# Moving the projections' SiLU multiplications from VectorE to GpSimd, with an extra ScalarE pass

## The reference

```python
x = x + ga * mamba(ln(x) * (1 + ca) + sa)              # A: conv, SiLU, a scan over 16 states
x = x + gb * moe_top2(ln(x) * (1 + cb) + sb)           # B: routed experts, width 64
x = x + ga1 * gated_delta(ln(x) * (1 + ca1) + sa1)     # C
x = x + gb1 * attention_moe(ln(x) * (1 + cb1) + sb1)   # D: attention, 8 dense experts, width 512
```

```python
def short_conv(x, w):          # w: 4 taps for each channel
    xp = jnp.pad(x, ((0, 0), (Kc - 1, 0), (0, 0))).transpose(0, 2, 1)
    y = lax.conv_general_dilated(xp, w[:, None, :], (1,), 'VALID', feature_group_count=w.shape[0])
    return jax.nn.silu(y.transpose(0, 2, 1))
q = short_conv(x @ Wq, conv_q)   # 8 heads of 128 channels
k = short_conv(x @ Wk, conv_k)   # 8 heads of 128 channels
v = short_conv(x @ Wv, conv_v)   # 8 heads of 32 channels
```

## Time and profile before

| | us |
|---|---|
| median of 3 executions | 2813.87 |
| lowest and highest | 2811.92, 2821.78 |
| span of the profiled execution | 2813.2 |
| PE busy | 2441.0 |
| DVE (VectorE) busy | 2212.7 |
| ACT (ScalarE) busy | 1200.1 |
| POOL (GpSimd) busy | 549.1 |

### The profile page before, as it was taken

How to read it: one execution, slowest core, us unless ns; L and a number is a source line. 1 busy time by engine, 2 the same in 40 slices (tenths; PEclk the granted TensorE clock), 3 DMA queues, 4 the chain that set the end, 5 groups by cost and what they waited for, 6 DMA issues and landing times.

```text
span 2813.2 us, 61085 instructions
## 1 busy us (share of the span) xinstructions
PE 2441.0 (87%) x22584; PEld 1893.0 (67%) x22584; DVE 2212.7 (79%) x5136; ACT 1200.1 (43%) x2697; POOL 549.1 (20%) x497
## 2 busy tenths in 40 slices
PE   3688989888898988989888898988989889898997
PEld 2466768667686766768667586766758667686776
DVE  6677897878879887787878879887887978879742
ACT  3332536344353543436444353543536444253512
POOL 2122221122222022121112222022121112222010
PEclk7789999999999999999999999999999999999998
DMA  4000000000000000000000000000000000000000
GB/s 132 4 2 3 7 4 1 8 3 8 3 7 2 3 8 3 7 3 4 5 3 8 3 7 2 3 8 3 7 3 5 4 3 8 3 7 2 1 6 3
DMA packets 24835, 21.46 MB, mean 8 GB/s; under 512 B 7218, under 2 KB 21571, under 8 KB 24531
## 3 DMA queue, kind: packets, MB, share of 16 engines
q1 hardware_dynamic: 24530, 17.26, 2.2%
HBM read 15.13 MB, written 2.13 MB: 6 GB/s over the span
## 4 chain that ended last, share of the span: by engine, by line
PE 32%; issue 32%; DVE 27%; POOL 4%; ACT 2%; DVEq 0%; POOLq 0%; ACTq 0%
DVE wide L1382 4%; DVE wide L1394 3%; PE banks L891 3%; PE banks L1198 3%; PE banks L1024 3%; PE banks L1188 3%; DVE wide L1402 3%; PE banks L1016 2%; PE banks L1052 2%; DVE inv L1570 2%; PE banks L1005 2%; DVE inv L1566 2%; PE banks L963 1%; PE banks L1065 1%; DVE inv L1557 1%
## 5 line engine op out<-in xcount | busy, mean ns | idle before, releaser
L1519 DVE SCALAR_TENSOR_TENSOR wide<-pad,conv,wide 128x256 f32<-128x256 f32 x864 | 370.0, 496 | 0.0
L561 POOL TENSOR_TENSOR wide<-wide 128x512 f32<-128x512 f32 x128 | 188.3, 1471 | 832.0 <-DVE wide L1402 472.0
L1394 DVE TENSOR_TENSOR_SCAN wide<-wide 128x1024 f32<-128x1024 f32 x128 | 292.9, 2288 | 1.9 <-ACT wide L667 0.3
L667 ACT ACTIVATE wide<-small,a_neg 128x255 f32<-128x255 f32 x512 | 216.0, 496 | 173.9 <-DVE wide L1394 173.0
L1044 PE MATMUL banks<-hideb,identb 128*128 128x512 bf16 x800 | 272.1, 403 | 0.0
L1188 PE MATMUL banks<-inv,up 128*128 128x256 f32 x1024 | 264.5, 387 | 0.0
L1198 PE MATMUL banks<-down,inv 128*128 128x128 f32 x2048 | 256.5, 276 | 0.0
L1198 PEld LDWEIGHTS banks<-down,inv 128*128 128x128 f32 x2048 | 248.7, 192 | 5.0
L796 ACT ACTIVATE inv<-banks,up1b 128x256 f32<-128x256 f32 x512 | 214.0, 480 | 52.0 <-PE banks L1188 51.5
L1024 PEld LDWEIGHTS banks<-inv,mats 64*64 64x64 f32 x5120 | 168.3, 139 | 63.9 <-issue 62.1
L1024 PEld LDWEIGHTS banks<-inv 64*64 64x64 f32 x5120 | 159.5, 135 | 67.4 <-issue 65.3
(11 more groups left out here) (280 smaller groups left out, 4933.4 us busy)
## 6 DMA issues: line engine op xcount, KB each, us to landing
gates_bc<-gate_rows SPq DMA_DIRECT2D x32, 128.0 KB, 2.9
x<-in_x SPq DMA_DIRECT2D x16, 128.0 KB, 2.1
up<-in_W SPq DMA_DIRECT2D x1, 2048.0 KB
out<-xn_y SPq DMA_DIRECT2D x16, 128.0 KB, 2.1
wide<-in_wmod SPq DMA_DIRECT2D x2, 384.0 KB, 5.6
con<-in_con SPq DMA_DIRECT2D x1, 724.0 KB, 4.7
w_k<-in_Wk SPq DMA_DIRECT2D x1, 512.0 KB
w_q<-in_Wq SPq DMA_DIRECT2D x1, 512.0 KB
```

The lines of the kernel that those rows point to most:

```text
L561: g.tensor_tensor(ypart[p % 2], r[:, 0:512], r[:, 512:1024], ALU.add).then_inc(a_yp.h, 1)
L667: last = s.activation(decay[st % 2][:, at + 1:at + T], dt[:, c, 1:T], ACT.Exp, scale=a_neg[:, c, st * SG + q:st * SG + q + 1])
L1394: v.tensor_tensor_scan(state[st % 2], decay[st % 2], drive[st % 2], 0.0, ALU.mult, ALU.add).then_inc(a_h.h, 1)
L1519: v.scalar_tensor_tensor(dst, src, w, dst, ALU.mult, ALU.add).then_inc(c_conv.h, 1)
```

## The change

The nine SiLU multiplications of each sample leave VectorE. GpSimd gets a `c_proj` of its own with them, as plain products of two tensors, and since a plain product cannot add the one, ScalarE adds it in a second instruction over the whole 128x512 tile, in place, which waits for its own tanh. The semaphore `c_th` counts to 18 instead of 9. On GpSimd the 12 steps of `c_proj` stand between `c_norm` and `c_gate`, so `c_gate` moves from the beginning of the stage to behind the last multiplication. The added wait of the next pass (`c_kq` in `a_norm`) is on GpSimd's own earlier work.

```diff
@@ TURNS
     "gpsimd": (
-        "yyxxyyyyyyxxxxxxxyxyxxyyxyxxx"),
+        "yyxxyyyyyyxxxxxxxyxyxxyyxyxxxxxxxxxxxxxxx"),
@@ signals
-        c_th = sig("c_tanh", 9); c_kq = sig("c_silu", 9); c_sq = sig("c_squares", 8)
+        c_th = sig("c_tanh", 18); c_kq = sig("c_silu", 9); c_sq = sig("c_squares", 8)
@@ gpsimd
                     g.wait_ge(mod_done, 1)
+                else:
+                    g.wait_ge(c_kq.h, c_kq.at(i - 1, 9))
...
+            def c_proj(i, m):
+                if 0 <= m - 3 < 9:
+                    n = m - 3
+                    if n == 0 and not isinstance(i, int):
+
+                        g.wait_ge(c_rms.h, c_rms.at(i - 1, 8))
+                    g.wait_ge(c_th.h, c_th.at(i, 2 * n + 2))
+                    g.tensor_tensor(kq[:, n] if n < 8 else v2, th1[n % 2], xc1[n % 3], ALU.mult).then_inc(c_kq.h, 1)
@@ scalar
                     s.activation(th1[m % 2], xc1[m % 3], ACT.Tanh, scale=0.5).then_inc(c_th.h, 1)
+                    s.wait_ge(c_th.h, c_th.at(i, 2 * m + 1))
+                    s.activation(th1[m % 2], th1[m % 2], ACT.Identity, bias=1.0).then_inc(c_th.h, 1)
@@ vector
             def c_proj(i, m):
-                if 0 <= m - 3 < 9:
-                    n = m - 3
-                    if n == 0 and not isinstance(i, int):
-
-                        v.wait_ge(c_rms.h, c_rms.at(i - 1, 8))
-                    v.wait_ge(c_th.h, c_th.at(i, n + 1))
-                    v.scalar_tensor_tensor(kq[:, n] if n < 8 else v2, th1[n % 2], 1.0, xc1[n % 3], ALU.add, ALU.mult).then_inc(c_kq.h, 1)
                 m -= 1
```

More of the change, by code:

```diff
@@ L606, in _ @@
             follow(g, TURNS["gpsimd"], dict(a_norm=a_norm, a_scan=a_scan, b_norm=lambda i: rstd(i, 1), b_root=b_root_, c_norm=lambda i: rstd(i, 2),
-                           c_gate=c_gate, c_gmask=c_gmask, c_roots=c_roots, c_unit=c_unit,
+                           c_proj=c_proj, c_gate=c_gate, c_gmask=c_gmask, c_roots=c_roots, c_unit=c_unit,
                            c_squares=c_squares, c_rms=c_rms_, d_norm=lambda i: rstd(i, 3)))
```

## The result

The change makes the kernel slower: 2903.52 us (median of 4, 2897.69 to 2908.35) against 2817.82 us (median of 4, 2811.92 to 2825.61). The ratio is 1.0304, with a 95% interval of 1.0279 to 1.0329, some 86 us. The span of the profiled execution went from 2813.2 to 2906.5 us. The forecast had the direction right and a size of 56 us.

What follows compares the result with a forecast made beforehand. TensorE, packed in the projections, was taken as the bound. 3.5 us for each of 15 passes (52.5) plus 3.6 for sample 0 made 56 us on the 2813.2 span, 2869.3, so 2870 us; range 2838 to 2903.

Steps and rivals of the forecast that it cites:

- 3.9 - 0.7 + 0.3 = 3.5 us a pass: Projections: later end of VectorE's last convolution, less delay taken up in the tail, plus waits of ScalarE and VectorE not coinciding.
- What bounds the kernel: Projections: TensorE packed, 32.00 of 32.00 us, VectorE nearly so; the start of the last sums of squares moves the pass's end.
- Part 2: GpSimd's products in the projections: eight fall on convolutions, each stopping VectorE 1.01 us; 8.1 us against 4.2 saved, 3.9 later.
- the upper bound: Most that one GpSimd product could cost VectorE: 1.27 us, the whole length of L561.
- The lower bound: Least that one GpSimd product could cost VectorE: nothing, if it always fell on a `d_mix` or a wait.
- Part 3: ScalarE in the projections: added instruction lengthens a step from 2.96 to 3.63 us, making ScalarE as full as VectorE.
- The rival in which ScalarE alone sets the pace: Projections: products meet no convolution, ScalarE costs 1.2 to 1.8 us a pass; about 2837 us, chance 0.13.
- the step without ReLUs: ScalarE between m = 5 and 6: the wait for the product is not hidden there, leaving about 0.5 us.
- Part 4: Last convolution's end to last sums of squares: 2.73 us becomes 2.0, taking up 0.7; 0.3 added back for waits.
- Part 5: `c_gate`, roots and masks after the projections: roots slip under 1 us against a cover of 3.7 us.
- Sample 0: Projections of the first sample, outside the 15 passes: 3.9 - 1.0 + 0.7 = 3.6 us slower, its tail growing.
- The rival's 2907 us: TensorE's clock falls in new projection gaps: some 5 us at low level cost 2.5 more, 6.0 a pass; chance 0.08.

Runs made afterwards that it cites:

- unread fills, no pass: Changed kernel with each GpSimd product replaced by fills that read nothing from SBUF, and ScalarE's added instruction left out: 2810.15 against 2819.56 us, 0.9974.
- the pass alone, warm: Kernel before plus only ScalarE's added instruction, products staying on VectorE, with 5 extra TensorE matmuls a sample holding the clock up: 2849.38 against 2819.56 us, 1.0115.
- unread fills and the pass: Changed kernel with each GpSimd product replaced by fills that read nothing from SBUF, ScalarE's added instruction kept: 2857.11 against 2819.56 us, 1.0129.
- products, no pass: Changed kernel with ScalarE's added instruction left out, so the one is not added: 2876.71 against 2813.81 us, 1.0217.
- fills reading one column, and the pass: Changed kernel with each GpSimd product replaced by fills and a tiny product reading one SBUF column: 2889.32 against 2813.81 us, 1.0268.
- changed, warm: Changed kernel plus 15 extra TensorE matmuls a sample ahead of the waits for squares, to hold the clock up: 2894.84 against 2819.56 us, 1.0267.
- changed, warm, second product let in: Changed kernel with 15 extra matmuls a sample, and VectorE made to wait within block 3's convolution for the second product: 2880.36 against 2817.61 us, 1.0208.
- changed, warm, products in halves: Changed kernel with 15 extra matmuls a sample, each GpSimd product cut in two of 128x256: 2911.57 against 2817.61 us, 1.0333.
- nine products more on the kernel before: Kernel before plus nine GpSimd products a sample, of constant tiles into a spare tile nobody reads: 2974.53 against 2813.81 us, 1.0570.
- the pass alone: Kernel before plus only ScalarE's added instruction, the product staying on VectorE as a plain product of two tensors: 2867.81 against 2813.81 us, 1.0199.

## Why the prediction was right about the direction and wrong about the size

In lengths at full clock, the runs give this account of a pass (the changed kernel itself has no pass without a low stretch):

| | us | over before |
|---|---|---|
| before | 35.87 | |
| unread fills, no pass | 35.87 | 0.0 |
| the pass alone, warm | 38.06 | 2.2 |
| unread fills and the pass | 38.08 | 2.2 |
| products, no pass | 39.04 | 3.2 |
| fills reading one column, and the pass | 39.91 | 4.0 |
| changed, warm | 40.86 | 5.0 |
| changed, warm, second product let in | 39.70 | 3.8 |
| changed, warm, products in halves | 41.42 | 5.5 |
| nine products more on the kernel before | 42.8 | 6.9 |

So a pass pays 2.2 us for ScalarE's added instruction, some 1.8 for GpSimd being held up by VectorE (39.91 - 38.08), some 1.0 for VectorE being stopped (40.86 - 39.91), and on top 42.56 - 40.86 = 1.7 for the low clock. The three differences are taken in this order, and another order would share out the 5.0 us a little differently. 5.0 x 15 = 75 us is what the passes of the warm kernel cost; its sample 0 costs 6.6 more, and its span is 85.3 us over the one before, though its median is 75. With the clock it is 6.7 x 15 = 100 us of length, plus 4.2 for sample 0, less the 15 us by which the stage between was shorter than before (120.3 against 121.3 us, 15 times): 89, against 93.3 of span. Of the 4 us left, 3 lie between the last sums and the next L1018.

**What failed** is the sum 3.9 - 0.7 + 0.3 = 3.5 us a pass, against 5.0 at full clock and 6.7 as it ran. The product that VectorE holds up stood in it at nothing and costs some 1.8 us. The tail stood in it with 0.4 us gained, and 0.6 were lost. ScalarE's added pass, 2.2 us by itself, had no term of its own. The low clock was left out of the sum, with a chance of 0.08, and costs 1.7 us.

**What bounds the kernel** was right and decided the direction: TensorE is packed, and VectorE's relief is worth nothing. The unread fills showed it to the hundredth of a microsecond.

**Part 2**, the exclusion, was right in kind and off in its working. One stop costs 1.02 us, where 1.01 was taken (6.2 us for six a pass). There were six a pass and not eight: the second product was not let in at all, and the last two fell behind the last group. L1525's mean came to 592 ns, not 629. The last group's end came 1369.36 - 1331.83 = 37.53 us behind the first projection against 33.15, 4.4 later where 3.9 was forecast. That nearness is luck: six stops less the 4.2 us saved are 1.9 us, and 1.58 us more is VectorE's wait behind the held-up product. The failed step is the upper bound: "1.27 above (the whole L561)" looked only at what a product costs VectorE, not at what VectorE costs a product. The lower bound, nothing on a `d_mix`, which reads PSUM, was not shown by a row but is shown here: the two `d_mix` instructions at 1348.53 took 0.60 us while the product of block 1 ran, and the longest L1701 of the run took 353 ns against a median of 342. A row for the other direction stood in the earlier trace rows: L561's longest took 3192 ns, behind a single scan of 2.28 us (in sample 0, at 44.51 us). Part 2 even read it in the earlier trace rows, where a scan made L561 0.54 us longer, but gave it no price in the sum.

**Part 3** failed in its size. It said that ScalarE becomes as full as VectorE, that its wait for the product "is hidden, except in the one step with no ReLUs", and priced no loss by the pass itself beside VectorE's. The pass alone costs 2.2 us a pass. The rival in which ScalarE alone sets the pace, 1.2 to 1.8 us, is the nearest estimate to it, and what was missing is that its term has to be added to the exclusion's and not run beside it. The half microsecond forecast for the step without ReLUs came true (0.46 us of waiting for the product at 1357.62), but a step with them had 1.65, ahead of block 4's tap, behind the held-up product.

**Part 4** was wrong in sign: from the last group's end to the last sums there were 1372.69 - 1369.36 = 3.3 us, not 2.0 + 0.3. ScalarE was behind by then, and began block 8's tanh only at 1370.50, 1.1 us after that convolution had ended. So 3.9 - 0.7 + 0.3 became 4.4 + 0.6 = 5.0.

**Part 5** held: the roots began 0.27 us behind their input, and the masks stayed ahead of TensorE. **Sample 0** cost 4.2 us where 3.6 was said.

**The clock.** It had a chance of 0.08. The gaps were 1.20 and 1.55 us and the clock fell behind them, in two passes behind the one of 1.20 alone. That the full clock followed the single gap of 1.52 us in the earlier trace rows was too little to build on. No length of a gap tells the cases apart: with the pass alone the clock fell in twelve passes behind gaps of 0.59 and 0.40 us and stayed up in three with the same gaps; with a gap of 1.50 us in every pass (the fills that read one column) it fell in five of fifteen. What the runs do show is that it never fell in the projections of the loop's passes in the six kernels whose gaps there were gone or at most 0.47 us (before, unread fills without the pass, and the four with extra matmuls). When it falls stays open. The rival's 2907 us is near the measured time, but that is luck, since its sum is not the measured one: 2.5 us a pass for the clock on 3.5, where the runs show 1.7 on 5.0. No run shows its term, 2.5 us for some 5 at the low level: the passes of the changed kernel had 5.6 us at 0.50 on average between first projection and last sums, for those 1.7.

What stays open: why it is always the second product of a pass (in sample 0, the first) that VectorE does not let in, while others get in within 0.2 us. It came in the third of three groups that followed back to back in the changed kernel, but later groups ran as close and let theirs in, and with nine products more on the kernel before the fourth was held up too (2.04 us). One instruction on GpSimd that adds and multiplies at once was not run, so the change without its pass is known only with the one left out.

## What to carry to other kernels

Before work is moved off a busy engine, ask whether that engine's share of the stage is what moves the end; here the queue of TensorE had no gap, and the prize was 0.26%. Where two engines exclude each other, price both directions, and follow the one that is held up to those who wait for it: the maximum of a row, and not its median, gives a first sign of that price. Where a stage was packed on TensorE, new gaps also put the clock at risk (1.7 us a pass in the changed kernel), and five to fifteen idle matmuls a sample ahead of the waits are a cheap way to find out how much that is.

## What the runs showed of the hardware

- In these runs exclusion went with reads. GpSimd's fills of 128x768 and 128x512, which read nothing, ran beside the same convolutions without a trace on either (0.74 and 0.52 us, groups of 2.46 us), while a GpSimd product of two tensors in SBUF stopped a convolution instruction for 1.02 us of its own 1.27.
- The one that waited could wait for long. A GpSimd instruction on 128x1 elements took 2.10 us in place of 0.19, and a product 3.26 to 3.92 in place of 1.27, until VectorE's run of convolutions had ended (by 0.06 us for the small one, by 1.13 to 1.14 for the products), though one convolution instruction takes 0.48 us. Elsewhere the wait was that of one instruction: the 3.19 us of L561 ended 1.07 us behind a single scan of VectorE.
- TensorE's granted clock fell to 0.50 of the full one for stretches of 3.4 or 6.8 us in a stage that was otherwise busy, after gaps of 1.20 and 1.55 us, but with the pass alone also after gaps of no more than 0.59 us; it fell in the projections of none of the 60 passes of the four runs with extra matmuls in the gaps. What a stretch of 3.4 us costs depends on where it lies: nothing where TensorE would have waited anyway (40.86 us in two passes of the changed kernel), 0.8 us early in the projections (39.91 against 40.7 us with the fills that read one column), 1.3 to 1.7 near their end (38.04 against 39.4 to 39.7 us with the pass alone).
